# A graph attention layer on one core: the first aggregate's halves ahead of the attention steps, and the line of left scores in parts of 4 and 12 tiles

## What is computed

```python
h = relu(layernorm(x))                        # 2048 x 256
type_sum = adj @ h                            # adj is 2048 x 2048, of zeros and ones
attn_a = sigmoid(concat([type_sum, h]) @ Wa.T + ba)
attn_b = sigmoid(concat([type_sum, h]) @ Wb.T + bb)
hs = h @ W_sa
s_left, s_right = hs @ a_sa[0, :256], hs @ a_sa[0, 256:]
scores = s_left[:, None] + s_right[None, :]
e = where(adj != 0, exp(-leaky_relu(scores, 0.01)), 0)
x_a = (e / (sum(e, axis=1) + 1e-5)) @ hs
x_b = (adj @ (h @ W_gcnb)) + b_gcnb           # made here as (adj @ h) @ W_gcnb
out = x + sigmoid(attn_a * x_a + attn_b * x_b)
```

## Time and profile before

| | |
|---|---|
| Median of 3 runs | 186.48 us (184.98 to 186.76) |
| The profiled execution | 184.32 us |
| Its span | 182.5 us |
| PE busy | 173.7 us (95%) |
| DVE busy | 146.7 us (80%) |
| ACT busy | 115.2 us (63%) |
| POOL busy | 18.3 us (10%) |
| Aggregates' matmuls (L776, two forms of 128) | 49.5 and 49.4 us |
| Attention products (L799 to L801, 272 each) | 71.0, 70.8 and 70.9 us |

### The profile page before, as it was taken

One profiled execution on the slowest core, in us unless ns is written; L12 is line 12 of the kernel. 1 busy time (PEld: TensorE's weight loads), 2 busy tenths in 40 slices (PEclk: granted clock), 3 DMA queues, 4 the chain that ended last, 5 costly groups with the idle time before them and its releaser, 6 DMA issues.

```text
span 182.5 us, 3402 instructions
## 1 busy us (share of the span) xinstructions
PE 173.7 (95%) x1323; PEld 126.3 (69%) x1323; DVE 146.7 (80%) x309; ACT 115.2 (63%) x169; POOL 18.3 (10%) x42
## 2 busy tenths in 40 slices
PE   7989999999919999999999999999999999999993
PEld 2646766744403447888874468888888888888892
DVE  3798897523699999979999970799999999987542
ACT  3597899530497998657756770295686586683410
POOL 4654426030000020000000000000000000000000
PEclk9999999999996999999999999999999999999999
DMA  5999699999970079500001010000010010011101
GB/s 139 286 246 182 188 182 192 229 225 236 341 297 0 4 115 224 120 4 0 2 4 57 0 57 0 4 0 0 4 57 0 5 57 0 4 59 45 72 30 29
DMA packets 5519, 16.87 MB, mean 92 GB/s; under 512 B 624, under 2 KB 1408, under 8 KB 4736
## 3 DMA queue, kind: packets, MB, share of 16 engines
q0 software_dynamic: 1584, 8.39, 24.1%
q1 hardware_dynamic: 3920, 8.27, 12.7%
HBM read 22.94 MB, written 2.11 MB: 137 GB/s over the span
## 4 chain that ended last, share of the span: by engine, by line
PE 82%; DMA 8%; ACT 4%; DVE 3%; issue 1%; DVEq 0%
PE ps L776 22%; PE ps L801 15%; PE ps L800 15%; PE ps L799 15%; PE ps L792 6%; DMA sl_row<-sl_line 6%; PE ps L841 3%; PE ps L756 3%; DMA sl_line<-part_b 3%; PE ps L743 2%; ACT z L373 1%; DVE z L565 1%; DVE agg_lo L546 1%; ACT e_hi L341 1%; ACT x_sb L336 1%
## 5 line engine op out<-in xcount | busy, mean ns | idle before, releaser
L799 PE MATMUL ps<-mv_lo,e_hi 128*128 128x257 f16 (+2 forms) x272 | 71.0, 267 | 0.0
L801 PE MATMUL ps<-mv_hi,e_lo 128*128 128x257 f16 (+2 forms) x272 | 70.9, 266 | 0.0
L800 PE MATMUL ps<-mv_hi,e_hi 128*128 128x257 f16 (+2 forms) x272 | 70.8, 266 | 0.0
L373 ACT ACTIVATE z<-z,log_e 128x1024 f32<-128x1024 f32 x32 | 36.7, 1146 | 33.7 <-DVE z L565 33.7
L776 PE MATMUL ps<-adj,nat_hi 128*128 128x512 f16 x128 | 49.5, 387 | 4.4 <-DVE agg_lo L546 3.8
L776 PE MATMUL ps<-adj,nat_lo 128*128 128x512 f16 x128 | 49.4, 386 | 0.0
L565 DVE SCALAR_TENSOR_TENSOR z<-sl_row,exs,far 128x512 f32<-128x512 f32 x64 | 45.0, 744 | 4.0 <-DMA sl_row<-sl_line 4.0
L573 DVE TENSOR_TENSOR e_lo<-z,e_hi 128x1024 f16<-128x1024 f32 x32 | 38.9, 1216 | 1.3 <-ACT e_hi L383 1.3
L383 ACT ACTIVATE e_hi<-z 128x1024 f16<-128x1024 f32 x32 | 33.3, 1041 | 0.0
L800 PEld LDWEIGHTS ps<-mv_hi,e_hi 128*128 128x128 f16 x272 | 26.5, 98 | 3.2
L799 PEld LDWEIGHTS ps<-mv_lo,e_hi 128*128 128x128 f16 x272 | 26.4, 97 | 3.3
(11 more groups left out here) (69 smaller groups left out, 174.0 us busy)
## 6 DMA issues: line engine op xcount, KB each, us to landing
adj<-in_adj_t POOLq DMA_DIRECT2D x6, 1024.0 KB, 9.9
x_sb<-in_x SPq DMA_DIRECT2D x6, 512.0 KB, 8.9
out<-res SPq DMA_DIRECT2D x7, 256.0 KB, 2.0
adj<-in_adj_t POOLq DMA_DIRECT2D x3, 512.0 KB, 8.1
sl_row<-sl_line SPq DMA_DIRECT2D x2, 512.0 KB, 8.6
x_sb<-in_x SPq DMA_DIRECT2D x3, 256.0 KB, 4.3
adj<-in_adj_t POOLq DMA_DIRECT2D x2, 256.0 KB, 6.1
wa_sb<-in_w_wide SPq DMA_DIRECT2D x1, 258.0 KB, 4.0
```

What stands on the lines that cost most here:

```text
L373: act.activation(z[:, n % ZRING, :, :], z[:, n % ZRING, :, :], ACT.Exp, bias=log_e[:, 0:1], scale=SLOPE - 1.0).then_inc(exp_done, 1)
L799: pe.matmul(ps[:, bank, cols], e_hi[:, s, i1], mv_lo[:, j, cols], start=(j == 0), stop=False)
L800: pe.matmul(ps[:, bank, cols], e_hi[:, s, i1], mv_hi[:, j, cols], start=False, stop=False)
L801: return pe.matmul(ps[:, bank, cols], e_lo[:, s, i1], mv_hi[:, j, cols], start=False, stop=(j == NT - 1))
```

## The change

The halves of aggregate 0 are made ahead of the attention steps: on ACT between `factor_l` and the second line copy, on DVE between the last `mv_lows` and `w_post_low`. The two places inside the loop over n go. The line is cut into tiles 0 to 3 and tiles 4 to 15 in place of two halves. The first transpose now stands in front of tile 6, in `wide(4)`, pass p = 3, and waits for the scores of pairs 0 and 1; its copy on ACT is in `mv_highs(3)`. Chunk 0 of the steps waits for the first part, and chunks 1 to 3 for the second. The order on SP and on POOL is the same.

```diff
-SL_UNIT = 6
+SL_PARTS = ((0, 4), (4, 16))
+SL_UNIT = 4
...
-        sl_turn = [part_b[0:NT // 2, h, 0:P] for h in range(2)]
+        sl_turn = [part_b[0:hi - lo, h, 0:P] for h, (lo, hi) in enumerate(SL_PARTS)]
...
             def sl_store(h):
+                lo, hi = SL_PARTS[h]
                 sp.wait_ge(sl_moved, h + 1)
-                sp.dma_start(sl_line[h * N // 2:(h + 1) * N // 2].rearrange("(t i) -> t i", i=P), sl_turn[h]).then_inc(sl_stored[h], 16)
+                sp.dma_start(sl_line[lo * P:hi * P].rearrange("(t i) -> t i", i=P), sl_turn[h]).then_inc(sl_stored[h], 16)
 
             def sl_spread(h):
                 sp.wait_ge(sl_stored[h], 16)
-                half = slice(h * N // 2, (h + 1) * N // 2)
-                sp.dma_start(sl_row[:, half], sl_line[half].partition_broadcast(P)).then_inc(sl_ready[h], 16)
+                part = slice(SL_PARTS[h][0] * P, SL_PARTS[h][1] * P)
+                sp.dma_start(sl_row[:, part], sl_line[part].partition_broadcast(P)).then_inc(sl_ready[h], 16)
...
             def sl_lines(h):
                 act.wait_ge(sl_turned, h + 1)
-                act.activation(sl_turn[h], ps[0:NT // 2, SL_BANKS[h], SL_COLS], ACT.Copy).then_inc(sl_moved, 1)
+                act.activation(sl_turn[h], ps[0:SL_PARTS[h][1] - SL_PARTS[h][0], SL_BANKS[h], SL_COLS], ACT.Copy).then_inc(sl_moved, 1)
...
             act.activation(factor_l[:, :], exs[:, :, SL], ACT.Exp, scale=SLOPE).then_inc(factors_done, 1)
+            agg_highs(0)
             sl_lines(1)
...
-                if n == 0:
-                    agg_highs(0)
...
-                    dve.wait_ge(sl_ready[c // 2], 16)
+                    dve.wait_ge(sl_ready[min(c, 1)], 16)
...
             mv_lows(NPAIR - 1)
+            agg_lows(0)
             w_post_low()
...
-                if n == 2:
-                    agg_lows(0)
...
             def sl_lines(h):
-                pe.wait_ge(exs_ready, 4 * h + 4)
-                pe.transpose(ps[0:NT // 2, SL_BANKS[h], SL_COLS], exs[:, h * NT // 2:(h + 1) * NT // 2, SL],
-                             ident[:, :]).then_inc(sl_turned, 1)
+                lo, hi = SL_PARTS[h]
+                pe.wait_ge(exs_ready, hi // 2)
+                pe.transpose(ps[0:hi - lo, SL_BANKS[h], SL_COLS], exs[:, lo:hi, SL], ident[:, :]).then_inc(sl_turned, 1)
```

## The result

| | before | changed |
|---|---|---|
| Median | 185.87 us (184.98 to 186.76, 4 runs) | 179.16 us (178.71 to 179.72, 4 runs) |
| Profiled execution | 184.32 us, span 182.5 | 178.80 us, span 177.0 |
| PE idle in front of aggregate 2 | 3.81 us | none |
| PE busy | 95% of the span | 97% |

The ratio is 0.9641 (95% interval 0.9575 to 0.9706). Between the two profiled executions 5.52 us went; the forecast had 5.56. Between the medians 6.7 went, 1.2 more.

The account below looks back on a forecast made before the run. PE, busy 95% of the span, was taken as the bound; 3.97 us of gap plus 1.59 of half clock gave 5.56, so 178.8 from the profiled execution. The forecast was 179.8, range 177.9 to 181.8.

Parts of the forecast that it names:

- Halves earlier, and the gap: Before aggregate 2: making aggregate 0's halves ahead of the steps removes PE's stall; 3.97 us for the gap.
- The clock's part: First 8 matmuls of aggregate 2 run at full instead of half clock; 1.59 us, bounds 0 and 1.59.
- The 2.16 us and the middle of two ends: Profiled execution lies 2.16 us below the median; forecast 179.8 taken as the middle of 178.8 and 180.9.
- the sum of 5.56: PE's whole gain around aggregate 2: 3.97 us for the gap plus 1.59 for matmuls at half clock.
- The adjacency of chunk 2: Start of aggregate 2: these loads land by some 49 us, so no new wait; cost taken as 0.
- The line: Start of the steps: earlier, smaller first spread lets z start at 42.84, 4.0 us sooner; insurance, no added gain.
- the margin of 1.0 us: Start of z: by turns of packets the first spread lands at 41.8, before DVE is ready at 42.84.
- E's readiness: Pair 0: step 7 ready at 70.3 and asked for at 75.19, slack 4.9 us.
- A: Clock stays low, or new 1 to 3 us wait at aggregate 2 or pair 0; 181.4 to 183; chance 0.05.
- B: PE's stall before aggregate 2 is for chunk 2's adjacency, not the aggregate; 184.3 to 186.5; chance 0.03.
- C: First spread lands late, steps and pair 0 slip; slower by 1% from landing 55.1, 190 at 57; chance 0.02.

Follow-up runs that it names:

- gap filled: Kernel before with 16 unused 128x512 matmuls on PE in front of aggregate 2; 183.30 us, ratio 0.990 to before.
- twice the runs: Changed kernel with the first part's spread as two DMAs of 2 tiles in place of one of 4; 179.68 us, ratio 0.972 to before.
- the longest gap: Changed kernel with PE waiting for E's third step before aggregate 2; 185.83 us, ratio 1.008 to before.

## Why the prediction was right, and where it was not

**Halves earlier, and the gap.** Right in mechanism and size. ACT's high half started at 38.51 (38.58 forecast), DVE's low half at 39.56 (39.5), aggregate 2 followed aggregate 1 without a gap. The halves alone give the same gain, so a change of the order on two engines is enough; the line alone gives it too, so the order was not the only way to free PE.

**The clock's part.** Right for the profiled execution (1.59 us), and shown by filling the gap. Its bounds, 0 and 1.59, were too narrow on one side: behind a gap 0.27 us longer it was 2.8 us. All 39 runs of the kernel before that stood beside the experiments, sorted by their mean granted clock:

| mean clock | runs | median us | range |
|---|---|---|---|
| 1.00 | 1 | 182.91 | |
| 0.988 to 0.991 | 26 | 184.5 | 183.96 to 186.24 |
| 0.979 to 0.981 | 12 | 185.9 | 185.38 to 186.68 |

The steps are 1.6 and 1.4 us. The profiled execution of before has a mean clock of 0.991 and belongs to the middle row.

**The 2.16 us and the middle of two ends.** This was the step that did not hold: the prediction found the profiled execution 2.16 us below the median, left open what the difference was, and split it to arrive at 179.8. Of the two ends the lower, 178.8, was the better one. Most of the 2.16 us lies in those few first runs, whose clocks are not on record: the median of the 39 runs is 184.72, only 0.4 above the profiled execution. In the same job the changed kernel gained 185.03 - 179.09 = 5.9 us, near the sum of 5.56. That 179.8 lies near 179.16 is in part the width of that split and not its reasoning.

What the slower of the runs of before lost is not shown, since no trace of one was kept. "How late the line lands", the prediction's own guess, fits. In two other profiled kernels, in which the line is made as before, its first half landed 0.3 and 0.4 us later against the end of aggregate 1 (halves only, and gap filled), which would make the gap 4.1 to 4.2 us; and a gap of 4.08 us cost 1.2 us more of clock than one of 3.81. The low clock at the start of the kernel is the rival: in the profile of the line alone it brought the mean clock to 0.981 by itself. The same gap with a larger loss of clock can't be excluded either.

**The adjacency of chunk 2.** Right: PE did not wait for it.

**The line.** ACT's copy in pass 3 pushed its `scale_a` by 0.12 us and cost nothing that the end shows. Store 0 was issued at 24.55 (24.6), the spread at 30.34 (29.7 to 31.5), and it landed at 41.1, near the bound of 41.8 and far from the 36.6 by bytes. The transfer took 10.8 us, more than the 10.25 that the bound had for it. In the second profile of the changed kernel it took 11.8 and landed some 0.3 us ahead of the first z, so the margin of 1.0 us was nearly used. The Trainium skill (DMA: Bandwidth & Descriptors, Queues, rings and completion order), by which the engines take turns by packets and not bytes, was the better guide here by that landing, though in the one execution with twice the runs they cost 1.5 times and not twice. Spread 1 was issued at 45.68 (47.8 forecast), since store 1 took less than the 6.9 us; the spread took 9.2 and landed at 54.9 (58.3 to 63.2), long before step 8. "The edit of the line adds nothing to the first edit" held. That it would have been enough alone was not in the prediction, though its own numbers say so: 54.74 - 4.00 = 50.74 against 50.81.

**E's readiness.** Step 7 was ready at 70.15 (70.3 forecast) and asked for at 75.23 (75.19). DVE's wait for the third `post` product, which was to swallow differences, was 6.5 us in the changed kernel and 2.1 with the halves alone, whose time is the same.

**Rivals.** A and B did not happen. C was made on purpose: with a landing at 53.8 the kernel is 0.8% slower than before (interval 0.4 to 1.2%), from about the landing that was named. Its account lacked step 4, `post(0)` and the clock. Its last figure is a slip: by its formula T = 57 gives 178.8 + 57 - 47.7 = 188.1 from the profile's sum, and not 190.

## What to carry to other kernels

When an engine waits, look at when the operands of the releasing instruction were ready: here at 35.6 us for an instruction that ran at 53.5, and its place behind the steps in a hand-written order was what held it. Test two edits one by one even if their sum comes out as forecast, because both may remove the same stall. Count a stall of TensorE with the matmuls at half clock behind it, and sort repeated runs by mean granted clock before explaining their spread. The sorting doesn't explain all of it: a run of the kernel before took 186.24 us at 0.991, and one with the gap filled 185.06 at 1.00. Don't set a forecast by the median of three runs when a profiled execution disagrees with it; take more runs.

## What the hardware showed that was not expected

- The clock's loss behind a gap comes in unequal sizes: in the profiles none behind 1.29 us, 1.6 us behind 3.81 and 2.8 us behind 4.08. Seven of the eight runs with the longest gap have a mean clock of 0.979 to 0.981. One run of the kernel before kept its clock at 1.00 and took 182.91 us.
- It also falls at the start in some executions. Two profiled ones in which PE waited 0.8 to 0.9 us for the constants near 6.5 us had it, with mean clocks of 0.981 and 0.990; the second profile of the changed kernel had a wait of 0.8 us there too and a mean clock of 1.00. What sets it off was not settled.
- A broadcast from DRAM to 128 partitions took 10.2 to 11.8 us for 128 to 512 KB beside the adjacency loads, but 7.0 for 512 KB and 9.2 for 768 KB issued at 47.8 and 45.7 us, when those loads were ending.
